# A four-layer gated transformer stack on one core: shorter runs of products that nobody reads

## The reference

```
x = x + tanh(g_xattn[0]) * L0_xattn(ln(x), ctx)   # self part, ln1, 8-head attention, ln2, relu MLP, ln3
x = x + tanh(g_ffn[0])   * L0_ffn(ln(x))          # token shift, sigmoid gate, squared relu
x = x + tanh(g_xattn[1]) * L1_xattn(ln(x), ctx)   # one head of 128
x = x + tanh(g_ffn[1])   * L1_ffn(ln(x))          # 16 experts, each takes its top tokens, plus a shared one
x = x + tanh(g_xattn[2]) * L2_xattn(ln(x), ctx)   # 16 heads of 16
x = x + tanh(g_ffn[2])   * L2_ffn(ln(x))          # see below
x = x + tanh(g_xattn[3]) * L3_xattn(ln(x), ctx)   # 16 heads of 64
x = x + tanh(g_ffn[3])   * L3_ffn(ln(x))          # ternary weights, 8-bit activations

# L0_xattn:
y = ln(x + sa, ln1_g, ln1_b);  y = ln(y + attn(y, ctx), ln2_g, ln2_b)
return ln(y + relu(y @ lin1.T + b1) @ lin2.T + b2, ln3_g, ln3_b)
# L2_ffn, two causal layers l = 0, 1:
x = x + causal_attn(ln(x, ln1_w[l], ln1_b[l]))
h = ln(x, ln2_w[l], ln2_b[l])
x = x + (token_moe if l == 0 else sequence_moe)(h)   # 8 experts, best 2, per token or per sequence
```

## Time and profile before

| what | value |
|---|---|
| runs | 1730.68, 1734.31, 1734.47 us |
| profiled execution | 1724.97 us, of which the span is 1723.4 us |
| mean granted TensorE clock | 0.961 of full |
| PE busy | 1594.9 us, 93% of the span |
| DVE, ACT, POOL busy | 741.0, 680.1, 240.4 us |

### The profile page before, as it was taken

How to read it: one execution, slowest core, us unless ns; L and a number is a source line. 1 busy time by engine, 2 the same in 40 slices (tenths; PEclk the granted TensorE clock), 3 DMA queues, 4 the chain that set the end, 5 groups by cost and what they waited for, 6 DMA issues and landing times.

```text
span 1723.4 us, 32899 instructions
## 1 busy us (share of the span) xinstructions
PE 1594.9 (93%) x12477; PEld 1322.6 (77%) x12477; DVE 741.0 (43%) x2621; ACT 680.1 (39%) x2160; POOL 240.4 (14%) x378
## 2 busy tenths in 40 slices
PE   7999989889999999999689988989999999999986
PEld 5787877689986777777488877878987777777765
DVE  2635445521025666755111137553114444344457
ACT  2614423322105757556133317543324443244432
POOL 2012200000001121211411123128000000000000
PEclk9999999989999999989699989889999999999998
DMA  9500011238601010400498920206850001000000
GB/s 324 195 1 2 1 40 37 85 108 304 139 1 52 11 44 2 176 2 2 157 321 300 318 97 23 99 31 217 300 175 1 1 1 37 1 2 1 2 1 22
DMA packets 103255, 156.41 MB, mean 91 GB/s; under 512 B 12231, under 2 KB 80959, under 8 KB 102535
## 3 DMA queue, kind: packets, MB, share of 16 engines
q1 hardware_dynamic: 97515, 143.53, 25.5%
q0 software_dynamic: 3552, 9.18, 1.6%
q10 hardware_dynamic: 2048, 1.84, 0.3%
HBM read 147.31 MB, written 11.67 MB: 92 GB/s over the span
## 4 chain that ended last, share of the span: by engine, by line
PE 66%; ACT 8%; DVE 5%; issue 3%; DMA 2%; POOL 1%; SPq 1%; DVEq 0%; ACTq 0%; POOLq 0%
PE psum L567 42%; PE psum L638 5%; ACT arena L839 5%; PE psum L622 4%; PE psum L662 4%; PE psum L916 3%; PE psum L523 3%; DMA moe_b<-in_moe_b 2%; POOL token_rows L1217 1%; PE psum L903 1%; PE psum L670 1%; DVE arena L756 1%; ACT arena L851 1%; PE psum L908 0%; SPq L985 0%
## 5 line engine op out<-in xcount | busy, mean ns | idle before, releaser
L839 ACT ACTIVATE arena<-arena,rowmin 112x375 f32<-112x375 f32 (+1 forms) x584 | 292.8, 508 | 179.3 <-DVE rowmin L756 179.1
L567 PE MATMUL psum<-arena,region 128*128 128x112 f32 (+2 forms) x1920 | 325.8, 328 | 6.5 <-DMA arena<-in_ctxT 2.5
L567 PEld LDWEIGHTS psum<-arena,region 128*128 128x128 f32 x1920 | 263.2, 197 | 69.8 <-issue 8.1
L567 PE MATMUL psum<-region,arena 128*125 128x128 f32 (+4 forms) x1632 | 234.4, 293 | 16.5 <-DVE arena L1986 4.8
L567 PEld LDWEIGHTS psum<-region,arena 128*125 128x125 f32 (+2 forms) x1632 | 197.2, 184 | 51.5 <-issue 19.3
L638 PEld LDWEIGHTS psum<-identity,arena 112*125 112x125 f32 (+1 forms) x1240 | 142.4, 177 | 63.7 <-ACT arena L851 17.2
L638 PE MATMUL psum<-identity,arena 112*125 112x112 f32 (+1 forms) x1240 | 169.2, 279 | 18.8 <-ACT arena L851 5.0
L567 PE MATMUL psum<-arena 128*128 128x128 f32 (+4 forms) x896 | 138.2, 312 | 0.8 <-DMA moe_b<-in_moe_b 0.8
L622 PE MATMUL psum<-arena 32*112 32x375 f32 (+3 forms) x912 | 133.5, 477 | 0.5 <-DVE arena L734 0.4
L567 PEld LDWEIGHTS psum<-arena 128*128 128x128 f32 (+2 forms) x896 | 124.0, 189 | 12.1 <-issue 1.6
L897 POOL COPY arena<-rinv 112x128 f32<-112x128 f32 x136 | 34.0, 293 | 595.2 <-DVE rinv L776 571.3
(11 more groups left out here) (298 smaller groups left out, 1871.3 us busy)
## 6 DMA issues: line engine op xcount, KB each, us to landing
stream<-in_moe_w SPq DMA_DIRECT2D x36, 1024.0 KB, 7.4
arena<-in_moe_w SPq DMA_DIRECT2D x36, 1024.0 KB, 7.3
arena<-in_ctxT SPq DMA_DIRECT2D x32, 375.0 KB, 4.0
stream<-in_e_wg SPq DMA_DIRECT2D x8, 512.0 KB, 4.4
stream<-in_e_wu SPq DMA_DIRECT2D x8, 512.0 KB, 5.5
stream<-in_e_wd SPq DMA_DIRECT2D x8, 512.0 KB, 6.6
region<-in_e_wg SPq DMA_DIRECT2D x8, 512.0 KB, 7.5
region<-in_e_wu SPq DMA_DIRECT2D x8, 512.0 KB, 8.2
```

The costliest lines, as they stand in the source:

```text
L567: last = pe.matmul(dst, l, r, start=(i == 0), stop=(i == n - 1))
L839: last = act.activation(e, e, ACT.Exp, bias=rowmin[:, j, n:n + 1], scale=-1.0, accum_out=rowsum[:, j, h:h + 1])
```

## The change

Nine places of PE's stream hold fewer products without a reader. Five calls in the source carry them: three `turn` calls and `turn_second` go from 14 to 6 (8 executions, since each runs for both turns), and the first turn of the second causal layer goes from 45 to 32. Nothing else is edited: no wait, no buffer, no order.

```diff
-                turn(pe, p, it, 1, 1, xn, 14)
+                turn(pe, p, it, 1, 1, xn, 6)
...
-                turn(pe, p, it, 2, 2, xn, 14)
+                turn(pe, p, it, 2, 2, xn, 6)
...
             def turn_second(it):
                 p = p_f[1]
-                keep_busy(pe, bank_t[3], 14)
+                keep_busy(pe, bank_t[3], 6)
...
-                    turn(pe, p, it, 0, (at_norm[NORM_A + it]) - it * p["normed"].times, first[it], 0 if it else ([0, 45][l]),
+                    turn(pe, p, it, 0, (at_norm[NORM_A + it]) - it * p["normed"].times, first[it], 0 if it else ([0, 32][l]),
...
-                    turn(pe, p, it, 1, (at_norm[NORM_A2 + it]) - it * p["normed"].times, [h[:, it, :] for h in hrow], 14)
+                    turn(pe, p, it, 1, (at_norm[NORM_A2 + it]) - it * p["normed"].times, [h[:, it, :] for h in hrow], 6)
```

## The result

The changed kernel took 1720.61 us in the median of five runs (1717.84 to 1724.92); the kernel before took 1733.53 us in five (1730.68 to 1734.47). The ratio is 0.9932, 95% interval 0.9915 to 0.9949: 11.8 us faster, between 8.8 and 14.7. In a later session, where both kernels ran some 10 us quicker, the same pair gave 0.9925 (0.9903 to 0.9947).

What follows compares the result with a forecast made beforehand. PE's stream was taken to bound the kernel, with readerless products on its path. Terms 3.76 + 3.1 + 2.6 + 2.8 = 12.3 us, less 1.7 for the clock, gave 10.6: 1734.3 to 1723.7 us, range 1718 to 1733.

Steps and rivals of the forecast that it cites:

- One product, 0.235 us on the path: In PE's stream, each product without a reader takes 0.235 us at full clock; 8 fewer end 1.88 us sooner.
- Cross-attention, 3.1 us: First cross-attention, four norms: lane 3's norm becomes the bound, gaining 0.5, 0.8, 0.8 and 1.0 us, 3.1 in sum.
- First causal layer, 3.76 us: First causal layer, both turns: ACT's copies start 1.88 us sooner without stalling, 3.76 us in two turns.
- `turn_second`, 2.6 us: Second causal layer: one-column products end sooner, transposes and ACT come 1.3 us sooner, 2.6 us in two turns.
- Begin, 2.8 us: Begin of the second causal layer: 13 fewer products bring the attention's products 2.8 us sooner, bounds 1.8 to 3.06.
- The clock, -1.7 us: Whole kernel: one more half-clock stretch costs 1.7 us, with bounds from -2.9 us to 8 falls.
- the rival of four falls: Cross-attention's four norms: one more half-clock stretch behind each, 6.8 us back, gain 5.5 us, 1728.8 us; chance 22%.
- second rival: Cited for transposes not covering the longer stretch; second in the list: nothing comes of it, 1733 us, 10%.
- The 9 us between the profiled execution and the median: Whole kernel: median 1734.31 us lies 9.3 us above the profiled 1724.97; the difference is carried over unchanged.
- The slower rival: All eight norms: two half-clock stretches follow each without the products, 23.2 us less 12.3, 1745 us; chance 6%.

Runs made afterwards that it cites:

- the norms alone: Eight norms hold 6 products instead of 14, begin of the second causal layer keeps 45, against the kernel before: 1711.87 us against 1723.41, ratio 0.9937.
- none at the causal layers: 0 instead of 6 products at the causal layers' four norms, against the changed kernel; measured ratio to the kernel before 0.9948 (0.9934 to 0.9963).
- the further cuts: Three more product runs cut against the changed kernel (36 to 16, 12 to 4, 20 to 10): 1706.43 us against 1723.34 before, ratio 0.9897.

## Why the prediction was right

The forecast was 10.6 us; the runs gave 11.8 (8.8 to 14.7) and 12.9 (9.1 to 16.7). The mechanism held: at all nine places the run of products set the time, and once it is cut the norm behind it does. The closeness of the number is in part luck: the terms were 0.9 us too large in sum (12.3 against 11.4 measured) and the clock, taken at 1.7 us, cost some 0.5 us by the clocks on record (below), and the two errors lean against each other. The intervals can't tell 10.6, 11.4 and 12.3 apart.

**One product, 0.235 us on the path.** Held: 22 instead of 14 moved L567 by 0.224 us for each.

**Cross-attention, 3.1 us.** Measured 3.17. The step that mattered was to see that the run's end isn't the bound once it is cut: lane 3's norm is, because all transposes stand ahead of lane 0's products in PE's order. Taking 8 x 0.235 for each norm would have given 7.5.

**First causal layer, 3.76 us.** Measured 3.19 to ACT's first copy, which came 1.6 us nearer to the run's start and not 1.9. The term was mis-sized by 0.3 us a turn: lane 0 is normed 1.47 us after the run's start, not 1.40, and the transposes' first half reaches ACT 0.45 us after it starts, not 0.24 after the run's end. That ACT wouldn't stall on lanes 2 and 3 held: 2.79 us as before.

**`turn_second`, 2.6 us.** Measured 2.23: the last group of one-column products waits for lane 2 and then takes 0.9 us for both lanes, while the prediction let only lane 3's 0.46 us stand behind lane 3's norm. The table ends at L1707. At the products behind it (L567) turn 0 has only 0.6 us of its 1.1 left, since half clock sets in at 1094.6 there (1095.7 before).

**Begin, 2.8 us.** Measured 2.81 in the profile and 2.4 (0.9 to 4.0) in the runs.

**The clock, -1.7 us.** The sum of the measured steps, 11.4, less 1.7 would be 9.7; the runs gave 11.8 and 12.9, intervals 8.8 to 16.7. So the expected fall did not show as a cost, though the intervals can't exclude it. In the later session the granted clock was 0.9617 on average in the changed kernel (six executions) and 0.9620 in the kernel before (23), by estimate 0.5 us; in the session of the result it was 0.957 to 0.958 in the changed kernel, and that of the kernel before is on record for the profiled execution alone, 0.961. No stretch at half clock followed any of the cross-attention's norms with 6 products in the five profiled executions that hold 6 at all four (the changed kernel twice, the norms alone, none at the causal layers, the further cuts), which speaks against the rival of four falls (5.5 us net, outside both intervals). The causal norm of turn 0 shows how a slow stretch eats a term: half clock began at 756.60, 4.9 us after the run's start, where before it began 7.4 us after the earlier trace rows, and of 1.6 us at ACT 1.2 were left at the attention's products.

```profile
756.60:763.40 6.80, 6.80 (x35) 6.70 (x36) 3.25 (x22) 3.75 (x13) 0.00 (x0) 0.50 0.00 0
```

By the Trainium skill (TensorE: Matmul & The Clock Gate, Part 4: PE-mode transpose) transposes don't count as PE-busy in the same way. The prediction took from this that they would not cover the longer stretch, so that the norms with 6 products would fall (its "second rival" there must be the rival of four falls, the first of its list). The measurement doesn't bear this out for 6: no fall behind these norms in five profiled executions. For 0, where falls came, it can't separate transposes from idleness.

**The 9 us between the profiled execution and the median.** I carried the difference over unchanged, and the medians moved by 12.9 us, so that held: the terms are times on PE's path, alike in both. Where the 9 us come from is open. The later sessions give a hint: there the kernel before took 1717 to 1728 us, and the profiled 1724.97 would be an ordinary execution. The two profiles of before and after therefore can't be subtracted as wholes, and the stall of 7.0 us comes on top.

**The slower rival** (the products hold the clock up everywhere) was wrong for 6 and right in kind for 0: there some 10 of 13 us are lost.

## What to carry to other kernels

A run of filler products ahead of a wait should end about when the first operand that PE needs is ready. Beyond that each one costs its full time (0.224 us here). With none at all the clock falls in some executions, which the best run hides and the median shows; between 0 and 6 nothing was measured. Where a later operand binds (lane 3 here), filler up to that point costs nothing on the path. Read both from the timeline: a transpose group without idle time ahead of it means that the run reaches past its operand, and the producer's end says by how much.

## What was not expected of the hardware

- Taking the filler away altogether cost about 10 us at the eight norms, more than the 7 us I had bounded by 1.7 us for four falls, and widened the spread of the times (19 us in twelve executions, against 7 in 23 of the kernel before on that chip). The mean granted clock fell from 0.9608 to 0.9552.
- The same program issued PE's products one by one, some 0.7 us apart, for 5 us in one execution, with nothing in the profile to wait for; the cause stays open.
- The unchanged kernel's median was 1733.53 us in the session of the result and 1723.3 to 1723.7 on three chips later, while the ratio of the change is the same (0.9932 and 0.9925). The chip of the first session isn't on record, so whether the chip makes the 10 us isn't shown.
